# A macaron block with a Mamba-2 scan on 8 cores: the prefix sums of the next quarter made early, and VectorE's waits on TensorE gathered into one per head

## The reference

```python
x = x + 0.5 * ffn(layernorm(x), W1, b1, ..., W2, b2)
x = x + attn(layernorm(x), ...)
x = x + 0.5 * ffn(layernorm(x), W1, b1, ..., W2, b2)
# inside attn: res + mamba2(layernorm(x)), then + mlp(layernorm(.))
# mamba2:
zxbcdt = x @ in_proj_w.T
xBC = silu(causal_conv4(xBC)); dt = softplus(dt + dt_bias); A = -exp(A_log)
# for every time step t, for each of 32 heads (64 wide, state 64):
h = h * exp(dt_t * A) + (dt_t * x_t) B_t
y_t = h C_t + D * x_t
y = rmsnorm(y * silu(z)) * norm_w
return y @ out_proj_w.T
```

## Time and profile before

| | us |
|---|---|
| runs of the kernel | 9083.74, 8917.51, 9069.07 |
| median | 9069.07 |
| the profiled execution's own time | 8917.51 |
| its span (slowest core, core 1) | 8915.9 |
| all cores' spans | 8882.1 to 8915.9 |
| PE busy | 5119.6 (57%) |
| DVE busy | 4592.9 (52%) |
| ACT busy | 1905.7 (21%) |

### The profile page before, as it was taken

One profiled execution on the slowest core, in us unless ns is written; L12 is line 12 of the kernel. 1 busy time (PEld: TensorE's weight loads), 2 busy tenths in 40 slices (PEclk: granted clock), 3 DMA queues, 4 the chain that ended last, 5 costly groups with the idle time before them and its releaser, 6 DMA issues.

```text
span 8915.9 us, 111187 instructions; the slowest of 8 cores (8882.1 to 8915.9 us)
## 1 busy us (share of the span) xinstructions
PE 5119.6 (57%) x22944; PEld 2261.0 (25%) x22944; DVE 4592.9 (52%) x12271; ACT 1905.7 (21%) x3892; POOL 60.0 (1%) x117
## 2 busy tenths in 40 slices
PE   0058988634444444446245335444449889888888
PEld 0023333212222122122122112222224334333333
DVE  2036566466465565564664664655642132456564
ACT  0024233211211211211112112112112212324232
POOL 2000000000000000000000000000000000000000
PEclk7579999855755655656557557556569999999999
DMA  9953334200200101102002002001014444343443
GB/s 180 203 157 119 123 116 126 93 1 1 65 1 13 54 1 32 35 1 66 1 1 65 1 1 65 1 25 42 1 43 136 133 133 138 121 133 123 125 130 125
DMA packets 191413, 653.24 MB, mean 73 GB/s; under 512 B 21296, under 2 KB 46128, under 8 KB 179504
## 3 DMA queue, kind: packets, MB, share of 16 engines
q1 hardware_dynamic: 174624, 590.46, 20.6%
q0 software_dynamic: 16176, 55.66, 4.3%
HBM read 629.62 MB, written 72.09 MB: 79 GB/s over the span
## 4 chain that ended last, share of the span: by engine, by line
PE 37%; DVE 36%; issue 14%; DMA 8%; DVEq 3%; ACT 3%; SPq 0%; ACTq 0%; POOL 0%; POOLq 0%
PE ps L242 37%; DVE arena L578 4%; DVE arena L573 4%; DVE arena L769 4%; DVE arena L1011 4%; DVEq L92 3%; DVE hstate L1022 3%; DVE arena L582 3%; DVE arena L979 2%; DVE arena L990 2%; DVE arena L961 2%; DVE arena L1098 2%; DMA arena<-wffn 1%; DMA cffn<-arena 1%; DMA arena<-wm 1%
## 5 line engine op out<-in xcount | busy, mean ns | idle before, releaser
L242 PE MATMUL ps<-arena,wk 128*128 128x512 f16 x15552 | 3543.5, 387 | 1077.4 <-DMA wk<-cffn 499.2
L242 PEld LDWEIGHTS ps<-arena,wk 128*128 128x128 f16 x15552 | 1512.7, 99 | 3100.8 <-issue 1434.2
L242 PE MATMUL ps<-arena 128*64 128x128 f16 (+1 forms) x1568 | 466.9, 298 | 1355.7 <-DVE arena L1011 1222.2
L1035 ACT ACTIVATE arena<-arena 128x128 f32<-128x128 f32 x1024 | 318.7, 311 | 2392.3 <-DVE arena L961 2392.3
L573 DVE SCALAR_TENSOR_TENSOR arena<-arena,prm,ps 128x512 f32<-128x512 f32 x512 | 382.3, 747 | 633.9 <-ACT arena L571 544.7
L242 PE MATMUL ps<-arena,ind 32*128 32x128 f16 x3072 | 484.7, 291 | 249.1 <-DVE arena L970 111.7
L242 PEld LDWEIGHTS ps<-arena 128*64 128x64 f16 (+1 forms) x1568 | 199.0, 127 | 1603.2 <-issue 1497.9
L970 DVE TENSOR_TENSOR arena<-arena,ps 64x128 f16<-64x128 f16 x1024 | 285.7, 279 | 371.0 <-PE ps L242 267.1
L961 DVE TENSOR_SCALAR arena<-ps,arena 128x128 f32<-128x128 f32 x1024 | 352.6, 344 | 233.6 <-DVE hstate L1022 109.3
L568 ACT ACTIVATE arena<-ps,prm 128x512 f32<-128x512 f32 x512 | 353.0, 690 | 525.4 <-DVE arena L578 520.6
L249 PE MATMUL ps<-iden,arena 32*128 32x32 f32 x96 | 15.8, 287 | 702.5 <-DVE arena L812 702.5
(11 more groups left out here) (117 smaller groups left out, 3471.3 us busy)
## 6 DMA issues: line engine op xcount, KB each, us to landing
wk<-cffn SPq DMA_DIRECT2D x512, 512.0 KB, 3.8
wk<-cm SPq DMA_DIRECT2D x256, 512.0 KB, 3.4
wk<-cip SPq DMA_DIRECT2D x136, 512.0 KB, 3.5
wk<-cop SPq DMA_DIRECT2D x64, 512.0 KB, 3.7
arena<-wffn POOLq DMA_DIRECT2D x16, 1024.0 KB, 15.9
cffn<-arena SPq DMA_DIRECT2D x16, 1024.0 KB, 9.7
arena<-wm POOLq DMA_DIRECT2D x16, 1024.0 KB, 13.0
cm<-arena SPq DMA_DIRECT2D x16, 1024.0 KB, 4.8
```

What stands on the lines that cost most here:

```text
L242: e.matmul(a, l, r, start=st, stop=sp, tile_position=tp),
L1035: sD[s] = B.E("s", lambda e, s=s: e.activation(Dex[s % 2], e1[s % 2], AF.Exp), waits=[(s_v, ve1[s])], inc=s_s)
```

## The change

Two edits. First, the prefix is put in a function `emit_prefix`. That of quarter 0 stays where it was; that of quarter `q+1` is emitted in slot 26 of quarter `q`, behind the DVE work of that slot. So that the matmuls of quarter `q` still read their own values, `cumhi16`, `cumlo16` and `expcum16` get a second buffer, used by odd quarters (`hl2`; `iden32` and `zer16` are cut to the part in use, and make room). Second, in the slot loop the waits on `s_t` are changed: `e1` waits for `tslot[s]` in place of `tD[s]`; `Cd`, the first `dx` and `evac` wait for `tslot[s]` alone; the first `dxw` and `G` lose their wait on `s_t`.

```diff
+        hiP = [cumhi16, hl2[0:32, 0:128]]
+        expP16 = [expcum16, hl2[0:32, 128:256]]
+        loP = [cumlo16, hl2[0:32, 256:384]]
...
+            def emit_prefix(qq, w_first):
+                IB = qq % 2
+                B.E("v", lambda e, qq=qq: e.tensor_scalar(
+                    acum, dtb[:, qq * 128:(qq + 1) * 128], Aneg, None, ALU.mult),
+                    waits=w_first, inc=s_v)
+                B.dr("v")
...
+            vset_ms[0] = emit_prefix(0, [(s_s, dt_done), (s_t, s_t.n), (s_s, sv4_prev)])
...
-                vv = B.E("v", lambda e, q=q: e.tensor_scalar(
-                    acum, dtb[:, q * 128:(q + 1) * 128], Aneg, None, ALU.mult),
-                    waits=[(s_s, dt_done)], inc=s_v)
...
+                vsetup = vset_ms[q]
...
                     if s < 32 and "srelu" not in DBG_SKIP:
                         bk = s % 2
-                        w0 = [(s_t, tD[s]), (s_s, sv1)]
+                        w0 = [(s_t, tslot[s]), (s_s, sv1)]
...
-                        w0 = [(s_t, tD[s])]
-                        if s >= 2:
-                            w0.append((s_t, tY[s - 2]))
                         vCd[s] = B.E("v", lambda e, bk=bk, s=s, qo=qo: e.tensor_tensor(
                             Cd16[s % 2], xbc[17][0:64, qo:qo + 128], ps[bk][0:64, 128:256],
-                            ALU.mult), waits=w0, inc=s_v)
+                            ALU.mult), waits=[(s_t, tslot[s])], inc=s_v)
...
-                        w0 = [(s_t, tTR[p]), (s_s, sv3)]
-                        if p >= 2:
-                            w0.append((s_t, tY[2 * p - 3]))
+                        w0 = [(s_t, tslot[s]), (s_s, sv3)]
...
                         w0 = [(s_s, sv2)]
-                        if p >= 2:
-                            w0.append((s_t, tH[p - 2]))
...
-                        w0 = [(s_s, sD[hh]), (s_v, vsp)]
-                        if hh >= 2:
-                            w0.append((s_t, tY[hh - 2]))
                         vG[hh] = B.E("v", lambda e, hh=hh: e.tensor_tensor(
                             G16[hh % 2], Dex[hh % 2], spm, ALU.mult),
-                            waits=w0, inc=s_v)
+                            waits=[(s_s, sD[hh]), (s_v, vsp)], inc=s_v)
...
-                            ALU.mult, ALU.add), waits=[(s_t, tY[hh])], inc=s_v)
+                            ALU.mult, ALU.add), waits=[(s_t, tslot[s])], inc=s_v)
...
+                    if s == 26 and q + 1 < DBG_NQ[0]:
+                        vset_ms[q + 1] = emit_prefix(
+                            q + 1, [(s_s, dt_done), (s_t, tD[0]), (s_s, sv4)])
```

More of the change, by code:

```diff
@@ L177, in build_program @@
     iden16 = al("iden16", [128, 128], F16)
-    iden32 = al("iden32", [128, 128], F32)
+    iden32 = al("iden32", [32, 32], F32)
     tri32 = al("tri32", [128, 128], F32)
     ind16 = al("ind16", [32, 4096], F16)
+    hl2 = al("hl2", [32, 384], F16)
     sel16 = al("sel16", [128, 64], F16)
@@ L185, in build_program @@
     zer32 = al("zer32", [32, 128], F32)
-    zer16 = al("zer16", [64, 128], F16)
+    zer16 = al("zer16", [64, 64], F16)
     zer16h = al("zer16h", [64, 64], F16)
@@ L260, in gd @@
                    waits=waits, inc=inc, inci=16)
-    yd(iden32[:, :], c_iden, inc=y_c)
+    yd(iden32[:, :], c_iden[0:32, 0:32], inc=y_c)
     yd(tri32[:, :], c_tri, inc=y_c)
@@ L641, in mamba_stage @@
         o = a16.take(NC16 * TT); yn = A16[:, o:o + NC16 * TT]; OFFS["yn"] = o
-        o = a16.take(2048); yq = A16[:, o:o + 2048]; OFFS["yq"] = o
-        o = a16.take(256); cumhi16 = A16[0:32, o:o + 128]; hiexp16 = A16[0:32, o:o + 256]
+        o = a16.take(256); cumhi16 = A16[0:32, o:o + 128]
         expcum16 = A16[0:32, o + 128:o + 256]
         o = a16.take(128); cumlo16 = A16[0:32, o:o + 128]
+        hiP = [cumhi16, hl2[0:32, 0:128]]
+        expP16 = [expcum16, hl2[0:32, 128:256]]
+        loP = [cumlo16, hl2[0:32, 256:384]]
+        o = a16.take(2048); yq = A16[:, o:o + 2048]; OFFS["yq"] = o
         o = a16.take(32); nthi16 = A16[:, o:o + 32]
@@ L698, in mamba_stage @@
         rms_prev = 0
+        sv4_prev = 0
         for sc in range(NTT):
@@ L780, in mamba_stage @@
             bc_done = max(conv_done[16], conv_done[17])
+            def emit_prefix(qq, w_first):
[4 more added lines that the diff above has]
+                B.dr("v")
+                B.E("v", lambda e: e.tensor_tensor_scan(
+                    cum, acum, zer32[:, :], 0.0, ALU.add, ALU.add), inc=s_v)
+                B.dr("v")
+                B.E("v", lambda e: e.tensor_tensor_scan(
+                    rvi[:, 127::-1], acum[:, 127::-1], zer32[:, :], 0.0, ALU.add, ALU.add), inc=s_v)
+                B.dr("v")
+                B.E("v", lambda e: e.tensor_tensor(rve, rvi, acum, ALU.subtract), inc=s_v)
+                B.dr("v")
+                B.E("v", lambda e, IB=IB: e.tensor_copy(hiP[IB], cum), inc=s_v)
+                B.dr("v")
+                vs = B.E("v", lambda e, IB=IB: e.tensor_tensor(
+                    loP[IB], cum, hiP[IB], ALU.subtract), inc=s_v)
+                B.dr("v")
+                return vs
+            vset_ms = {}
+            vset_ms[0] = emit_prefix(0, [(s_s, dt_done), (s_t, s_t.n), (s_s, sv4_prev)])
             vdx_prev = {}
@@ L824, in mamba_stage @@
                 sv3 = B.E("s", lambda e: e.activation(dttm, ps[2][:, 64:96], AF.Copy), inc=s_s)
-                sv4 = B.E("s", lambda e: e.activation(expcum16, cum, AF.Exp),
+                sv4 = B.E("s", lambda e, q=q: e.activation(expP16[q % 2], cum, AF.Exp),
                           waits=[(s_v, vsetup)], inc=s_s)
@@ L891, in mamba_stage @@
                         t_mm(bk, ps[bk][:, 0:128], ind16[:, s * 128:(s + 1) * 128],
-                             cumhi16, start=True, stop=False, waits=w0)
+                             hiP[q % 2], start=True, stop=False, waits=w0)
                         t_mm(bk, ps[bk][:, 0:128], ind16[:, s * 128:(s + 1) * 128],
-                             cumlo16, start=False, stop=True)
+                             loP[q % 2], start=False, stop=True)
                         t_mm(bk, ps[bk][:, 128:256], ind16[:, s * 128:(s + 1) * 128],
-                             expcum16, start=True, stop=True, inc=s_t)
+                             expP16[q % 2], start=True, stop=True, inc=s_t)
                         tD[s] = s_t.n
@@ L1027, in mamba_stage @@
                                     ALU.mult, ALU.add),
-                                    waits=([(s_t, tH[p]), (s_s, svA)] if par == 0 else []),
+                                    waits=([(s_t, tslot[s]), (s_s, svA)] if par == 0 else []),
                                     inc=s_v)
@@ L1113, in mamba_stage @@
             vyn = s_v.n
+            sv4_prev = sv4
             for dc in range(NC8):
```

## The result

The changed kernel is slower. Its fastest run takes 9221.12 us where the kernel before has 8917.51, and the ratio is 1.036, with a 95% interval of 1.020 to 1.053: clear of no change, though the interval's lower end only just reaches 2%. The medians of all runs are 9380.93 and 9069.07 us. The forecast was 9234 us.

What follows compares the result with a forecast made beforehand. It took waits between engines, the DVE-PE round trip in the slot loop, to bound the kernel. From 8917.5 us, changed waits add 375 and the moved prefix takes off 59, giving 9234 us; range 9110 to 9400.

Steps and rivals of the forecast that it cites:

- Which wait ends last: Slot loop: DVE and PE make a round trip; in odd slots only `e1` is useful DVE work under PE's.
- What one wait costs: DVE gaps: each wait costs 0.07 us behind a `dr`, less or nothing where it passes under a running instruction.
- The odd slot: `e1` waits for H, starting 1.76 us after `G` instead of 0.47; `Cd` comes 0.98 us later.
- The even slot: Removed waits shorten `e1` to `G` from 2.19 to 1.93 us, gaining 0.26; a pair becomes 6.20 from 5.48.
- The quarter's head: From `yn` to the next quarter's `e1`: moving the prefix away gains 3.93 us in 24 of 32 quarters.
- The prefix in slot 26: Prefix of 2.39 us delays slot 27's `e1` to 3.24 us after `G`; 1.48 us stays as cost.
- Slots 32 and 33: End of the slot loop: they wait for H instead of Y1, ahead of states that wait anyway; not counted.
- The sum: Whole kernel: 8917.5 + 375 - 59 = 9234 us, 3.5% more.
- B: Rival on the slot loop: removed waits give nothing, so 116 us of gain are missing; 9350 us, chance 0.08.
- C: Rival on odd slots' `e1`: waits behind `tslot` are free once it comes, 108 us less; 9126 us, chance 0.12.
- D: Rival on odd slots: the move of `e1` is hidden, leaving a gain of 175 us; 8743 us, chance 0.08.

Runs made afterwards that it cites:

- `v1_e1_early`: The changed kernel with `e1` waiting for `tD[s]` again and `Cd` for Y1 alone; 8745.30 us, 0.980 of the fastest run before.
- `waits_more`: The kernel before with three more waits ahead of `dxw` from the third pair on, all on a value already reached; 9012.34 us.
- `tslot_last`: The changed kernel with `e1`'s four waits reordered, `tslot[s]` last in place of first; 9122.06 us, 99 us less than the changed kernel.
- `prefix_only`: The kernel before with the early prefix (slot 26, second buffers) and all its old waits; 8887.42 us, against 8906.44 for the kernel before.

## Why the prediction was right, step by step

**Which wait ends last.** Right. DVE and PE go back and forth once a slot, and `e1` was the only work of DVE under PE's matmuls in an odd slot. `v1_e1_early` puts it back there and the loss turns into a gain.

**What one wait costs.** Right: 0.07 us from the gaps of slots 0 and 2, and `waits_more` measures 0.45 - 0.24 = 0.21 for three. `tslot_last` shows the other half of it, that waits behind the one that comes last are gone through one by one: 0.21 for three. The reading of the Trainium skill (VectorE: DVE Perf Modes, "The DRAIN you can't avoid") by which such gaps are free doesn't hold for waits here.

**The odd slot.** Right. `e1` was forecast at 1.76 after `G` and is at 1.74, `Cd` at 2.28 and is at 2.26, the next `e1` at 4.27 and is at 4.19. The difference is `G`: I kept 0.25 between `Cd` and `G`, and with one wait less it is 0.21; the states come 0.02 earlier as well.

**The even slot.** Forecast 1.93 from `e1` to `G`; the changed kernel has 1.92 (3161.82 to 3163.74 in its timeline). A pair: forecast 6.20, measured 6.14 in the median, so 0.66 more than before and not 0.72.

**The quarter's head.** Forecast gain 3.93, measured 3.84, 3.79 in the mean. One term was missed: `tslot[0]` also counts the transpose of x, so slot 0's `e1` waits for it too (1.46 idle put down to `p L250`). `prefix_only`, whose `e1` waits for D alone, needs a median of 2.46 us from `yn`'s end to `e1`, the changed kernel 2.68 to 2.71.

**The prefix in slot 26.** Forecast `e1` at 3.24, measured 3.23; cost 1.48 and 1.49.

**Slots 32 and 33.** They were put at nothing, on the ground that the states wait for H anyway. That step was wrong: `evac` of slot 33 stands ahead of the states and now waits for H. `G` and that `evac` before, and in the changed kernel:

```profile
3254.81 0.29 DVE L1002 TENSOR_TENSOR arena<-arena 128x128 f16<-128x128 f32 x1 [0.31 <-DVE hstate L1022]
...
3256.10 0.35 DVE L1011 SCALAR_TENSOR_TENSOR arena<-arena,prm,ps 64x128 f16<-64x128 f16 x1 [0.74 <-PE ps L242]
...
3231.18 0.29 DVE L1007 TENSOR_TENSOR arena<-arena 128x128 f16<-128x128 f32 x1 [0.24 <-DVE hstate L1027]
...
3232.70 0.35 DVE L1016 SCALAR_TENSOR_TENSOR arena<-arena,prm,ps 64x128 f16<-64x128 f16 x1 [0.99 <-PE ps L243]
```

It starts 1.52 after `G` in place of 1.29, and the gate begins 0.24 later in the median: 32 x 0.24 = 8 us.

**The sum.** The forecast difference was 375 - 59 = 316 us, and 304 us lie between the fastest runs, 323 us between the medians of cores 4 to 7. The stretch from the first `e1` to the last grew from 4755.7 us to 5063.5 us (core 6 in both), 308 us. It is made up of 348 us in the slot loops without the prefix, where I had 375 (a pair is 0.66 longer and not 0.72); of -54 us for the moved prefix, where I had -59; of 8 us in slot 33, where I had nothing; and of some 6 us outside the loops that I can't put down to a line. So the mechanism and the large terms were right, and that the sum came within 12 us owes something to a term too large and others left out, which pull opposite ways.

**The rivals.** B, that removed waits give nothing, is refuted by `prefix_only` and `v1_e1_early`, whose slot loops differ in the removed waits alone: 2823 and 2670 us, 153 us less (142 us between their fastest runs, of different sessions). C is refuted by `tslot_last`. D named the gain that would be left if `e1` were hidden, 8743 us; the changed kernel doesn't do that, but `v1_e1_early`, built to, took 8745.30. The agreement owes something to luck: D counted the prefix in slot 26 at the price it has when `e1` waits anyway (1.48), and without that cover it is about 2.5 (24 x 1.0 = 25 us more). Against it a pair lost 0.06 us beyond the 0.26 of the even slot (14 x 32 x 0.06 = 27 us).

## What to carry to other kernels

Waits that are gathered into the one that comes last save an instruction each, but the earliest of the operations must then wait for what only the last one needs: look for the operation that used to run under the other engine's work, and leave its wait alone. Where an instruction has several waits, put the one that will come last at the end of the list. And before waits on another engine are thinned out, take away the engine's waits on itself that protect nothing: here they were worth 567 us, nearly four times the 153 us that the removed waits on PE gave.

## What the runs showed that was not expected

A DVE wait on its own last instruction costs more than its gap suggests. Behind the two state updates the gap read 0.38 us, but with the two `dr` gone `e1` starts 0.64 us earlier: without a `dr` between them the next instruction starts before the last one has ended (`e1` at 3102.40, the states' last end at 3102.48), and its four waits leave no gap there. The expectation had put 0.25 us on these two `dr`, from the gaps alone.
